# A two-block transformer kernel: how the first attention's negated maxima reach all partitions, and who splits the queries

## What is computed

```
x = x + attention1(layernorm(x))    # 16 heads of 64, position rows added to the keys, softmax, output projection
x = x + ffn_block(layernorm(x))     # attention of 16 heads of 8, layernorm, a router that picks one of
                                    # 4 experts (128 -> 512 -> 128), layernorm
```

```
qkv = x @ W_qkv + b_qkv
k = k + pos_enc
scores = einsum('bqhd,bkhd->bhqk', q, k) / scale
attn = softmax(scores, axis=-1)
out = einsum('bhqk,bkhd->bqhd', attn, v)
```

## Time and profile before

| | us |
|---|---|
| median of three executions | 2255.26 (2247.64 to 2261.68) |
| the profiled execution's own time | 2247.04 |
| its span, first to last instruction | 2245.2 |
| around the span | 1.8 |

### The profile page before, as it was taken

The page is one execution under the profiler, slowest core; times in us unless marked ns, Lnnn a source line. Parts: engine busy times, 40 slices in busy tenths (PEclk is TensorE's granted clock), DMA queues, the critical chain, the costliest instruction groups (busy, mean ns, idle before and its releaser), DMA issues.

```text
span 2245.2 us, 35828 instructions
## 1 busy us (share of the span) xinstructions
PE 2099.1 (93%) x12074; PEld 934.2 (42%) x12074; DVE 1741.8 (78%) x2794; ACT 1757.7 (78%) x2387; POOL 1226.4 (55%) x763
## 2 busy tenths in 40 slices
PE   5899999999999999999999999899999999999997
PEld 2444444444444444444444443333333333333334
DVE  5677777787787777777777775789999999999913
ACT  1588888888888888888888888268878888888882
POOL 1477777777777687687687688332113025006003
PEclk8799999999999999999999999679999999999998
DMA  3000000000000000000000000000000000000000
GB/s 119 1 1 1 1 1 1 1 1 1 1 1 1 1 1 1 1 1 1 1 1 1 1 20 1 1 1 1 2 1 1 2 1 6 2 2 6 1 1 10
DMA packets 12270, 11.30 MB, mean 5 GB/s; under 512 B 2112, under 2 KB 10944, under 8 KB 11968
## 3 DMA queue, kind: packets, MB, share of 16 engines
q1 hardware_dynamic: 12096, 9.01, 1.3%
HBM read 7.69 MB, written 1.05 MB: 4 GB/s over the span
## 4 chain that ended last, share of the span: by engine, by line
PE 61%; DVE 16%; ACT 13%; issue 6%; POOL 1%; DVEq 0%; ACTq 0%; POOLq 0%
PE acc_o L523 11%; PE acc_o L644 10%; PE scores L630 9%; PE scores L493 8%; ACT prob L830 6%; DVE mxp L1343 5%; PE ring L468 5%; DVE accp L1377 5%; ACT scores L838 3%; DVE mxp L1449 3%; ACT prob L861 2%; PE ring L689 2%; PE ring L610 2%; PE ring L697 2%; PE ring L542 2%
## 5 line engine op out<-in xcount | busy, mean ns | idle before, releaser
L1008 POOL TENSOR_TENSOR accp<-accp,prob 128x1024 f32<-128x1024 f32 x318 | 809.1, 2544 | 61.7 <-ACT prob L830 22.4
L1343 DVE TENSOR_REDUCE mxp<-ring 128x1 f32<-128x512 f32 x1024 | 648.1, 683 | 176.0 <-PE ring L468 166.3
L861 ACT ACTIVATE prob<-scores 128x512 f32<-128x512 f32 x1024 | 544.1, 599 | 136.0 <-PE scores L630 133.7
L830 ACT ACTIVATE prob<-scores 128x1024 f32<-128x1024 f32 x512 | 520.0, 1016 | 132.0 <-PE scores L493 109.5
L493 PE MATMUL scores<-q_all,k_all 64*128 64x512 f32 x3072 | 556.8, 408 | 6.4 <-ACT scores L838 4.9
L1449 DVE TENSOR_REDUCE mxp<-ring 128x1 f32<-128x512 f32 x789 | 510.1, 683 | 50.2 <-PE ring L610 34.2
L838 ACT ACTIVATE scores<-minus_all 128x1024 f32<-128x1024 f32 x510 | 524.5, 1029 | 26.3
L523 PE MATMUL acc_o<-prob,v 128*64 128x512 f32 x2048 | 497.4, 606 | 0.0
L468 PE MATMUL ring<-k_all,q_all 64*128 64x512 f32 x1024 | 412.3, 438 | 56.2 <-DVE q_all L1329 24.4
L493 PEld LDWEIGHTS scores<-q_all,k_all 64*128 64x128 f32 x3072 | 340.3, 186 | 64.1 <-ACT scores L838 26.1
L630 PE MATMUL scores<-q_all,k_all 32*128 32x512 f32 x1024 | 304.7, 494 | 13.0 <-ACT prob L861 8.8
(11 more groups left out here) (189 smaller groups left out, 1657.4 us busy)
## 6 DMA issues: line engine op xcount, KB each, us to landing
w_all<-w_pairs SPq DMA_DIRECT2D x1, 1344.0 KB, 11.1
pos_sb<-pos SPq DMA_DIRECT2D x1, 1024.0 KB, 5.8
w_sb<-w SPq DMA_DIRECT2D x4, 256.0 KB, 4.6
mrow<-m_rows SPq DMA_DIRECT2D x64, 2.0 KB
w_all<-w SPq DMA_DIRECT2D x1, 1024.0 KB, 5.4
q_all<-m_rows SPq DMA_DIRECT2D x64, 2.0 KB
out<-ff SPq DMA_DIRECT2D x4, 256.0 KB, 2.2
wout_sb<-wout_pairs SPq DMA_DIRECT2D x1, 512.0 KB, 7.6
```

What stands on the lines that cost most here:

```text
L830: nc.scalar.activation(prob[:, T % SLOTS1, :, :], sc[T % 2][:, :, :], ACT.Exp, scale=SCALE1).then_inc(exp_done, 1)
L861: nc.scalar.activation(prob2[:, h // 2, T % 2, h % 2, :], sc2[place % 3], ACT.Exp, scale=SCALE2).then_inc(exp2_done, 1)
L1008: nc.gpsimd.tensor_tensor(accp[:, k % 2], accp[:, k % 2], prob[:, T % SLOTS1], ALU.add).then_inc(pool_acc, 1)
L1343: done(nc.vector.reduce_max(mxp1[k % 2][:, h * QT + q, kc:kc + 1], bank[:], AX.X), ("max", k, q, kc, h))
```

## The change

1. The `minus` matmuls and the ScalarE copies to `minus_all` go. SyncE writes `m_rows` to a row in DRAM (`m_dram`), waits for that, and reads it back with one DMA that repeats it over all 128 partitions into `minus_all`, which now has two buffers. The first two tiles of the whole attention keep the matmuls against `mrow`, which is filled once.
2. ScalarE writes the biased projection of the queries to SBUF (`qf`) and frees the bank. VectorE makes both parts from `qf`: a copy to `qhi`, and, after a wait for that copy, a subtraction to `qlo`.
3. Last items by steps: 0 none, 1 `Q`, 2 `sums` (in the last chunk still 1), 3 `fin`, 4 `K` or `V`, 5 none, 6 `K` or `V`, 7 `y`. The inverses of the sums go to steps 3, 4 and 5 (the last two quarters together); `mred` to the start of step 3; GpSimd splits the first keys after its add of tile 10, not 8. `EARLY1` is 10, not 8.

```diff
-EARLY1 = 8
+EARLY1 = 10
 def last_item1(k, j):
-    if j == 1 and k > 0:
+    if j == 1 and k + 2 < CHUNKS1:
+        return ("Q", k + 2)
+    if j == (2 if k < LAST1 else 1) and k > 0:
         return ("sums", k - 1)
-    if j == 2 and k + 2 < CHUNKS1:
-        return ("Q", k + 2)
-    if j in (3, 6) and k // NC + 1 < PAIRS:
+    if j in (4, 6) and k // NC + 1 < PAIRS:
-    if j == 4 and k + 1 < CHUNKS1:
+    if j == 3 and k + 1 < CHUNKS1:
         return ("fin", k + 1)
-    if j == 5 and k + 1 < CHUNKS1:
-        return ("minus", k + 1)
 def recip_quarters(k, j):
-        return [j - 2] if 2 <= j < 2 + QT else []
+        return {3: [0], 4: [1], 5: [2, 3]}.get(j, [])
...
 # ScalarE
-            def rounded_queries(k):
+            def queries(k):
+                if k > 0:
+                    act.wait_ge(ql_ready, k)
                 wait_full(act, ("Q", k))
-                nc.scalar.activation(qhi[:, c, :], ring[bank_of(("Q", k))][:], ACT.Identity,
-                                     bias=bqk_all[:, p, 0:1]).then_inc(qh_ready, 1)
+                nc.scalar.activation(qf[:], ring[bank_of(("Q", k))][:], ACT.Identity,
+                                     bias=bqk_all[:, k // NC, 0:1]).then_inc(free[bank_of(("Q", k))], 1)
             def seed(T):
                 if T % NT < 4:
-                    for h in range(2):
-                        wait_free(act, ("minus", T // NT, h))
+                    act.wait_ge(m_spread, 16 * (T // NT + 1))
...
 # GpSimd
-                    if t == 8 and last_item1(k, 3) and last_item1(k, 3)[0] == "K":
-                        split_keys(*last_item1(k, 3)[1:])
+                    if t == 10 and last_item1(k, 4) and last_item1(k, 4)[0] == "K":
+                        split_keys(*last_item1(k, 4)[1:])
...
 # SyncE, for each chunk k, after fin(k)
+                if k == 0:
                 for h in range(2):
-                    sp.dma_start(mrow[64 * h:64 * h + 1, k % 2, :].bitcast(F32), ...).then_inc(m_dma, 16)
+                    sp.dma_start(mrow[64 * h:64 * h + 1, :].bitcast(F32), ...).then_inc(m_row, 16)
+                sp.dma_start(m_dram[k % 2].rearrange("(a n) -> a n", a=2 * QT), m_rows[0:2 * QT, :].bitcast(F32)).then_inc(m_out, 16)
+                sp.wait_ge(m_out, 16 * (k + 1))
+                if k >= 2:
+                    sp.wait_ge(seeded, NT * (k - 1) - 2)
+                sp.dma_start(minus_all[:, k % 2].rearrange("p h n -> p (h n)"),
+                             m_dram[k % 2:k % 2 + 1, :].to_broadcast([128, 2 * CW])).then_inc(m_spread, 16)
...
 # VectorE
             def q_proj(k):
-                bank = open_(("Q", k))
-                dve.wait_ge(qh_ready, k + 1)
-                done(nc.vector.scalar_tensor_tensor(qlo[:, c, :], bank[:], bqk_all[:, p, 0:1], qhi[:, c, :].bitcast(F32),
-                                                    ALU.add, ALU.subtract), ("Q", k))
+                wait_free(dve, ("Q", k))
+                nc.vector.tensor_copy(qhi[:, c, :], qf[:]).then_inc(qh_ready, 1)
+                dve.wait_ge(qh_ready, k + 1)
+                nc.vector.tensor_tensor(qlo[:, c, :], qf[:], qhi[:, c, :].bitcast(F32), ALU.subtract).then_inc(ql_ready, 1)
```

More of the change, by code:

```diff
@@ L138, in start1 @@
             + [("K", 0, 2)] + tiles[1] + [("K", 0, 3), ("V", 0, 2), ("V", 0, 3)] + tiles[2] + [("Q", 1)] + tiles[3]
-            + [("rows",)] + early[:3] + [("fin", 0)] + early[3:] + [("minus", 0)])
+            + [("rows",)] + early[:3] + [("fin", 0)] + early[3:])
 def uses1():
@@ L147, in use @@
             uses.extend([("max", *it[1:], h) for h in range(2)])
-        elif it[0] == "minus":
-            uses.extend([(*it, h) for h in range(2)])
         else:
@@ L402, in build @@
         order2 = [it for it in USES if it[0] in ("K2", "Q2")]
+        m_dram = nc.dram_tensor("m_dram", [2, 2 * CW], F32, kind="Internal").ap()
         block = ctx.enter_context(nc.Block())
@@ L499, in scores @@
                     return
-                if t < 2:
-                    pe.wait_ge(m_dma, 32 * (k + 1))
+                if t == 0:
+                    pe.wait_ge(m_row, 16 * 2)
                 for h in range(2):
-                    nc.tensor.matmul(sc[u][:, h, :], onesw[half(h), :], mrow[half(h), k % 2, :],
+                    nc.tensor.matmul(sc[u][:, h, :], onesw[half(h), :], mrow[half(h), :],
                                      start=False, stop=True).then_inc(sc_ready[u], 1)
-            def minus(k):
-                pe.wait_ge(m_dma, 32 * (k + 1))
-                for h in range(2):
-                    bank = begin(("minus", k, h))
-                    end(nc.tensor.matmul(bank[:], onesw[half(h), :], mrow[half(h), k % 2, :], start=True, stop=True),
-                        ("minus", k, h))
             def values(T):
@@ L563, in item1 @@
                     sums(it[1])
-                elif kind == "minus":
-                    minus(it[1])
                 else:
@@ L744, in _ @@
                     pe.wait_ge(pairs_dma, 16 * 3)
[L745 to L748, removed]
                 item1(it)
+            pe.wait_ge(blank, 4)
+            scores(0)
+            scores(1)
             for k in range(CHUNKS1):
@@ L834, in seed @@
                 if T % NT < 4:
-                    for h in range(2):
-                        wait_free(act, ("minus", T // NT, h))
+                    act.wait_ge(m_spread, 16 * (T // NT + 1))
                 act.wait_ge(exp_done, T - 1)
[L838 to L846, removed]
+                nc.scalar.activation(sc[T % 2][:, :, :], minus_all[:, T // NT % 2], ACT.Copy).then_inc(seeded, 1)
             def copy_o1(k):
@@ L929, in _ @@
                 elif it[0] == "Q":
-                    rounded_queries(it[1])
+                    queries(it[1])
             exps(0)
             exps(1)
-            minus_copy(0)
             seed(2)
@@ L953, in _ @@
                         sums_copy(it[1])
-                    elif it and it[0] == "minus":
-                        minus_copy(it[1])
                     elif it and it[0] == "Q":
-                        rounded_queries(it[1])
+                        queries(it[1])
                     for it in LATE1.get((k, j), []):
@@ L1248, in _ @@
                 wait_free(sp, ("fin", k))
-                for h in range(2):
-                    sp.dma_start(mrow[64 * h:64 * h + 1, k % 2, :].bitcast(F32),
-                                 m_rows[QT * h:QT * (h + 1), :].bitcast(F32)).then_inc(m_dma, 16)
+                if k == 0:
+                    for h in range(2):
+                        sp.dma_start(mrow[64 * h:64 * h + 1, :].bitcast(F32),
+                                     m_rows[QT * h:QT * (h + 1), :].bitcast(F32)).then_inc(m_row, 16)
+                sp.dma_start(m_dram[k % 2].rearrange("(a n) -> a n", a=2 * QT), m_rows[0:2 * QT, :].bitcast(F32)).then_inc(m_out, 16)
[4 more added lines that the diff above has]
+                             m_dram[k % 2:k % 2 + 1, :].to_broadcast([128, 2 * CW])).then_inc(m_spread, 16)
                 if k == CHUNKS1 - 2:
@@ L1354, in fin @@
                 if k > 0:
-                    dve.wait_ge(m_dma, 32 * k)
+                    dve.wait_ge(m_out, 16 * k)
+                if k == 1:
+                    dve.wait_ge(m_row, 16 * 2)
                 bank = open_(("fin", k))
@@ L1635, in _ @@
                 for j in range(STEPS1):
-                    if j == STEPS1 - 4 and k + 1 < CHUNKS1:
+                    if j == STEPS1 - 5 and k + 1 < CHUNKS1:
                         mred(k + 1)
```

20 lines of the change are left out of this document (10 added, 10 removed).

## The result

| | before | after |
|---|---|---|
| median, us | 2258.11 (2247.64 to 2261.68, 4 runs) | 2329.68 (2327.49 to 2333.49, 4 runs) |
| ratio | | 1.033 (1.029 to 1.037) |
| span of the profiled execution | 2245.2 | 2325.7 |
| copies that end the chunks, first to last | 123.7 to 1418.7 | 130.7 to 1501.2 |
| one chunk (that range / 31) | 41.8 | 44.2 |

The change makes the kernel 3.3% slower. The forecast was 2285 with a range to 2308, so the measured median lies 22 us above the range. The direction held, and so did the mechanism up to TensorE's new wait; what that wait does to TensorE's clock was missing. Of the 80.5 us that the span grew, 75.5 lie between the first and the last of the chunks' copies (1370.5 against 1295.0), 7.0 ahead of the first and -2.0 behind the last: nearly all of it is in the chunks of the first attention.

A forecast was written before the change was run, and what follows sets the result against it. TensorE's order, busy 93% of the span, was taken as the bound. A chunk gained 1.0 us net, +30 over 30 chunks, plus 1 for start and end: 2255 + 31 = 2286, rounded to 2285, range 2203 to 2308.

The forecast's parts named there:

- `minus` gone: Step without an item: two matmuls, a TensorE wait and two ScalarE copies go, 5.55 to 4.1 us, saving 1.4 per chunk.
- The two DMAs hidden: DRAM store and read back take 4.4 us of 11.3 before ScalarE's seed in step 6, so they cost nothing.
- `sums` a step later: With `sums` in step 2, VectorE's add is long done, so TensorE's 0.50 us wait per chunk goes.
- The wait for the split is moved, not removed: The 0.79 us bank wait goes; step 2's fourth max tile waits for VectorE instead, 3 to 4 us per chunk.
- Which course: Copy waits for GpSimd, or subtraction misses a 0.2 us gap: fourth max tile at 763.1; otherwise 760.6. The later was taken.
- The sum: Values of step 6 at 782.1 against 781.14: 1.0 us more per chunk, +30 us over 30 chunks.
- Start and end: Two more couples made ahead cost 2.5 us, partly regained in a late chunk and by earlier seeds: together +1 us.
- Rival A: Split after step 1: subtraction gets its turn at once, 1.6 us less per chunk, 2208 us; chance 0.31.
- Rival B: Split: the copy waits, but both parts then run in one turn, saving about 1.1 us per chunk, 2222 us; chance 0.06.
- D: DRAM row arrives late: 13 us for two landings, ScalarE waits 1.7 us per chunk, +50 us; chance 0.05.
- E: ScalarE becomes the bound, busy 35.6 of 41.8 us per chunk; called no rival of weight, no chance given.
- C: Turns shift between chunks, half running each course: -9 us, near 2246, no change that can be told; chance 0.11.

The follow-up runs named there:

- The DRAM row alone: Kernel before with only the negated maxima's way changed, through a DRAM row instead of `minus` matmuls and copies: 2210.14 us, ratio 0.983.
- short adds: Changed kernel with GpSimd's adds of tiles 4 to 6 of each chunk but the last cut to 8 of 512 columns, sums incomplete: 2199.56 us, ratio 0.979.
- The split alone: Kernel before with only the new queries' split (ScalarE to `qf`, VectorE copies and subtracts), projection still in step 2: 2376.96 us, ratio 1.058.
- the 384 columns: Changed kernel, ScalarE writing `qhi` and `qf`, plus an unneeded 384-column VectorE reduction ahead of the subtraction: 2323.30 us, ratio 1.033.
- with the wait filled: Changed kernel with step 2's third max matmul repeated 12 times before its signal: 2285.88 us, ratio 1.017.
- the change with the old split: Changed kernel with the queries' split as before (ScalarE rounds from the bank, one VectorE instruction reads and frees it): 2190.39 us, ratio 0.975.
- ScalarE writing both parts: Changed kernel with ScalarE writing both `qhi` and `qf` from the bank, VectorE only subtracting: 2209.17 us, ratio 0.983.
- 256 and 384 columns: The 256 run: changed kernel, ScalarE writing `qhi` and `qf`, plus an unneeded 256-column VectorE reduction ahead of the subtraction: 2222.89 us, ratio 0.989.
- 512 columns: Changed kernel, ScalarE writing `qhi` and `qf`, plus an unneeded 512-column VectorE reduction ahead of the subtraction: 2329.29 us, ratio 1.037.

## Why the prediction went wrong

By its own steps:

1. *`minus` gone, 1.4 us per chunk.* The DRAM row alone gave 41.8 - 40.6 = 1.2 us per chunk. Right but for 0.2, and the step without an item took as much more in the changed kernel (826.76 to 831.10, 4.34 us) than the 4.1 counted.
2. *The two DMAs hidden, with 5 us to spare.* Right: 4.8 us of 11.3, no wait. The low end of the bounds was the nearer one.
3. *`sums` a step later, 0.5 us.* Right, with 0.6 measured, of which 0.1 stays unexplained.
4. *The wait for the split is moved, not removed; VectorE and GpSimd take turns, a waiting instruction goes first.* Right in every link. The forecast had 8.9 us from the values of step 1 to those of step 2; it was 8.8. The copy, alone 0.43 us, did wait for its turn. The Trainium skill's statement ("SBUF — State Buffer", "Who interferes with whom") that such a copy can be blocked by GpSimd agrees with the traces: 0.43 us beside short adds, 1.10 beside full ones.
5. *Which course.* Either a turn for the copy or a slip of 0.1 to 0.2 us was said to be enough. The split alone (copy 504 ns, subtraction 2732) and the 384 columns show the second of these by itself; in one chunk of the split alone the subtraction was up at 835.98, 0.18 us behind GpSimd's next add.
6. *The sum: the step with `sums` 5.02 us at full clock.* **This is the step that failed.** The sum added the wait and then took every later step from rows in which TensorE ran at full clock. But behind the 3.3 us wait it ran at the lower level, and that step took 6.5 us. Measured: a chunk of 44.2 us against the 42.8 forecast; with the wait filled, 42.8 us. The difference of 1.45 us times 31 is 45 us. The mechanism was right, and one term was missing from it. That the forecast's chunk and the one with the filled wait agree so closely is in part luck: at full clock the step with `sums` took 4.78 us, 0.24 less than counted, and `fin` (4.49) and the step without an item were 0.17 and 0.24 over.
7. *Start and end, +1.* In the change with the old split, whose `EARLY1` is 10 as well, the first chunk's copy came at 122.0, 1.7 ahead of before. In the changed kernel it came at 130.7; the first chunk has a split and a stop of its own (4.46 us). Both ends together brought +5.0.

On the profiled execution the forecast was 2278 and the time 2327.5, a miss of 49.5 us: 45.5 in the chunks, most of it the clock, and 4 at the ends. The medians lie only 45 us apart, since the median before was put 8 us above the profiled execution and the median after lies 2 above its own; the near match with the clock's 45 us is chance.

Rival A's course was real. ScalarE writing both parts realised it, in a kernel that I didn't have in mind, with a chunk of 40.5 us where A had 40.2. That the times meet (2209.17 us, 2208 counted) is luck: A was counted down 47 us from 2255, and this kernel is 38.5 below 2247.67. A's condition, the moment against the next add, is what the runs with 256 and 384 columns straddle. Rival B came about in a single chunk: at 1248.84 the copy took 1.10 us, GpSimd's next add was late (up at 1250.09), the subtraction, up at 1249.97, took 0.69, and TensorE waited 1.3 us. D and E didn't come about: the row wasn't late, and ScalarE waited for TensorE. C didn't either: the same pattern of turns came in 29 of 30 chunks.

The trace before held a warning that I passed over. In the steady part TensorE never waited longer than 0.9 us, and the clock stood at 1.00. All costs of the forecast were taken from that state, while the forecast itself put a wait of 3 to 4 us into each chunk, outside of anything those rows cover. The range should have reached up by the price of TensorE's work just behind such a wait at half speed: one group of values matmuls, 1.94 us more, 58 us in 30 chunks, an upper end near 2366.

What stays open: when a stop makes the clock fall, here. Waits up to 0.9 us in each chunk of the kernel before went without it. Waits near 2.75 us (the split alone, 384 and 512 columns) and of 3.3 us had it in most chunks, and so had one of 2.22 us (with 384 columns, at 188.92, the values matmuls behind it 2.69 us). But the two of 3.33 us above, one of 2.73 us in the split alone (885.41) and one of 2.60 us with the wait filled (186.78) went without, with values matmuls of 1.94 us. So the length of the stop alone doesn't decide it, and no run here separates what else does.

## What to carry to other kernels

A bank that is freed earlier gains nothing when the reader behind it becomes slower: follow the in-order engine until the next buffer it must free. An instruction that reads one operand from PSUM and one from SBUF kept out of GpSimd's way here (749 to 752 ns in all 32 chunks of the kernel before; the one at 764.11 ran across the end of one GpSimd add and the start of the next), where the same work from SBUF alone didn't (median 2718 ns); moving a source from PSUM to SBUF next to a busy GpSimd is a change of its own and wants its own test. When a forecast puts a long stop into TensorE's stream, price the work behind the stop at the lower clock too: here 1.7 us in a chunk where the clock fell.

## What the runs showed of the hardware that was not expected

- The granted clock fell to its lower level in 27 of 30 chunks over the work behind a TensorE wait of 3.3 us or more and came back within the chunk (0.54 in the 3.27 us behind one wait, 0.96 over 333 us). In two chunks the same wait left it at 1.00. With the wait filled by useless matmuls it stayed at 1.00 from 540 to 873 us, and the kernel was 44 us faster.
- VectorE and GpSimd locked into a fixed rhythm: where a VectorE add that waited for GpSimd ends, GpSimd's next add runs, so the gaps between adds came at the same place in chunk after chunk. In one chunk each of the kernel before, the changed one, and those with both parts by ScalarE, 256 and 384 columns, GpSimd's add ended 3.43 to 3.45 us after the start of VectorE's add of step 1 (before: 755.76 to 759.19). The gap is some 0.15 us wide, and 0.13 us of VectorE work decided over 100 us.
